# Experts' results scattered to token rows and loaded as plain rows, and a third pair of score banks

## The reference

```python
x = _layernorm(x + _L0_attn_ref(x, ...))            # 16 heads of 64, causal
x = _layernorm(x + _L0_xattn_ref(x, ctx, mask, ...))
x = _layernorm(x + _L0_ffn_ref(x, ...))             # 8 experts, 2 for each token
x = _layernorm(x + _L1_attn_ref(x, ...))            # 16 heads of 16, causal, gates, rotations, an inner MLP
x = _layernorm(x + _L1_xattn_ref(x, ctx, ctx, ...))
x = _layernorm(x + _L1_ffn_ref(x, ...))

def _L0_ffn_ref(x, gate_w, dense_1_w, dense_1_b, dense_2_w, dense_2_b):
    gate = xf @ gate_w
    weights, sel = jax.lax.top_k(gate, k=2)
    weights = jax.nn.softmax(weights, axis=-1)
    h = swiglu(jnp.einsum('ecd,td->tec', dense_1_w, xf) + dense_1_b[None])
    y = jnp.einsum('edf,tef->ted', dense_2_w, h) + dense_2_b[None]
    y_sel = jnp.take_along_axis(y, sel[:, :, None], axis=1)
    return jnp.einsum('tkd,tk->td', y_sel, weights)
```

## Time and profile before

| | |
|---|---|
| median of 3 runs | 1195.58 us (1195.24 to 1195.78) |
| the profiled execution, its own time | 1197.88 us |
| its span, first to last instruction | 1196.1 us |
| busy: PE, DVE, ACT, POOL | 1098.9, 718.9, 551.1, 474.6 us |
| mean granted clock of TensorE | 0.97 of full speed |
| first block / experts / last block | about 0 to 474 / 474 to 699 / 699 to 1196 us |

### The profile page before, as it was taken

How to read it: one execution, slowest core, us unless ns; L and a number is a source line. 1 busy time by engine, 2 the same in 40 slices (tenths; PEclk the granted TensorE clock), 3 DMA queues, 4 the chain that set the end, 5 groups by cost and what they waited for, 6 DMA issues and landing times. The chain is left out here.

```text
span 1196.1 us, 20449 instructions
## 1 busy us (share of the span) xinstructions
PE 1098.9 (92%) x6772; PEld 792.6 (66%) x6772; DVE 718.9 (60%) x2197; ACT 551.1 (46%) x1399; POOL 474.6 (40%) x551
## 2 busy tenths in 40 slices
PE   9899989998999897999999988699899999998997
PEld 4476557645754676999999965455555665575875
DVE  1482376247524846555655647749849787956367
ACT  1381255217421834333333328367476557643542
POOL 0160034006400885666666547515432442323023
PEclk9999999999999899999999989589999999999999
DMA  6000200020002014951111135000100100000001
GB/s 209 19 1 1 60 19 2 0 60 19 1 0 61 2 61 144 323 163 46 50 49 45 45 110 185 6 1 9 28 1 17 36 2 26 10 1 19 1 1 36
DMA packets 39997, 55.85 MB, mean 47 GB/s; under 512 B 6758, under 2 KB 32166, under 8 KB 39894
## 3 DMA queue, kind: packets, MB, share of 16 engines
q1 hardware_dynamic: 30598, 39.61, 10.1%
q0 software_dynamic: 3408, 9.31, 2.8%
q10 hardware_dynamic: 5888, 5.64, 1.5%
HBM read 43.76 MB, written 10.78 MB: 46 GB/s over the span
## 5 line engine op out<-in xcount | busy, mean ns | idle before, releaser
L1821 PE MATMUL bank<-words 128*128 128x256 f32 (+3 forms) x872 | 268.3, 459 | 17.7 <-ACT words L2428 3.3
L1821 PEld LDWEIGHTS bank<-words 128*128 128x128 f32 (+1 forms) x872 | 163.9, 194 | 96.0 <-issue 58.9
L464 PE MATMUL bank<-words 128*128 128x512 f32 x384 | 171.1, 594 | 0.2 <-issue 0.2
L409 POOL TENSOR_TENSOR words<-words 128x256 f32<-128x256 f32 (+1 forms) x128 | 102.5, 830 | 152.7 <-DVE words L1090 152.2
L1297 PEld LDWEIGHTS bank<-words 128*128 128x128 f32 x1248 | 145.8, 192 | 3.5 <-ACT words L1333 1.6
L1297 PE MATMUL bank<-words 128*128 128x128 f32 x1248 | 146.3, 276 | 0.9 <-ACT words L1333 0.9
L787 ACT ACTIVATE words<-words 128x128 f32<-128x128 f32 (+1 forms) x256 | 112.9, 443 | 33.5 <-DVE words L923 33.5
L464 PEld LDWEIGHTS bank<-words 128*128 128x128 f32 x384 | 71.0, 190 | 78.5 <-issue 78.2
L779 ACT ACTIVATE words<-bank 128x512 f32<-128x512 f32 x48 | 28.7, 597 | 177.8 <-PE bank L464 177.8
L1348 ACT ACTIVATE words<-words 128x1024 f32 x39 | 41.1, 1057 | 137.1 <-PE bank L1297 113.2
L913 DVE COPY words<-bank 128x512 f32<-128x512 f32 x48 | 33.2, 691 | 91.9 <-PE bank L464 91.6
(11 more groups left out here) (366 smaller groups left out, 2050.8 us busy)
## 6 DMA issues: line engine op xcount, KB each, us to landing
words<-in_w SPq DMA_DIRECT2D x8, 1024.0 KB, 9.9
y_slots<-words ACTq DMA_DIRECT2D x39, 128.0 KB, 1.7
words<-in_w SPq DMA_DIRECT2D x8, 512.0 KB, 10.1
words<-in_x SPq DMA_DIRECT2D x4, 512.0 KB, 4.2
x_rows<-words SPq DMA_DIRECT2D x16, 128.0 KB, 1.8
words<-in_wm SPq DMA_DIRECT2D x2, 1024.0 KB, 7.2
out_x<-words SPq DMA_DIRECT2D x16, 128.0 KB, 1.8
words<-in_xt SPq DMA_DIRECT2D x3, 512.0 KB, 3.9
```

The source lines that it names most:

```text
L409: last = pool.tensor_tensor(part, part, inv[:, j % SLOTS0, :, t:t + 1].to_broadcast([P, 2, P * (t + 1)]), ALU.mult)
L464: last = pe.matmul(bank[c % 2][:, :], w, r, start=k == 0, stop=k == KD - 1)
L1821: last = pe.matmul(out, w, r, start=i == 0, stop=i == len(pairs) - 1)
```

## The change

The results no longer stay in slot order. A new table `home` gives for each slot the row of `y2` to which its result goes: a token's first choice goes to row RETURNED + token, its second choice to 2048 rows further. The one-hot tables carry RETURNED (6144) or RETURNED + 2048 besides the token's number, so `source` is the number's low eleven bits, and empty slots go to rows of their own below RETURNED.

POOL scatters each tile's 128 rows with an indirect transfer, behind `copy_values(j + 2)`; ACT issues no store. The product of gate and sigmoid moves from POOL to DVE. DVE's slot numbers and `base` fall away. At the end of the experts POOL no longer waits for the stores; SP does, at the head of the last block. Rows come back by plain loads of 128 rows on SP's queue, those of groups 0 and 1 early, and POOL's gathers fall away.

In the second half of group 0's attention the units rotate over three pairs of banks, 0 and 1, 2 and 3, 6 and 7. The turned rows of group 1, which had banks 6 and 7, go to banks 5 and 7. The third pair is used in no other place.

```diff
+RETURNED = -(-SLOTS // (B * S)) * B * S
...
-            for v, pattern, step in ((lane, [[1, P]], 0), (number, [[1, SLOT_TILES]], 0), (token, [[P, TILES]], 1), (index, [[1, 1]], 1)):
+            for v, pattern, step in ((lane, [[1, P]], 0), (number, [[1, SLOT_TILES]], 0), (index, [[1, 1]], 1)):
                 pool.iota(v[:, :], pattern=pattern, base=0, channel_multiplier=step, allow_small_or_imprecise_dtypes=True)
+            pool.iota(token[:, :, :], pattern=[[B * S, 2], [P, TILES]], base=RETURNED, channel_multiplier=1, allow_small_or_imprecise_dtypes=True)
...
-                dve.tensor_tensor(keep["base"][:, :], end[:, :], length[:, :], ALU.subtract)
...
-            dve.tensor_copy(keep["source"][:, :], bank[0][:, 0:SLOT_TILES]).then_inc(routed, 1)
+            dve.tensor_copy(keep["source"][:, :], bank[0][:, 0:SLOT_TILES])
+            dve.drain()
+            dve.tensor_scalar(keep["source"][:, :], keep["source"][:, :], B * S - 1, None, ALU.bitwise_and).then_inc(routed, 1)
+            dve.tensor_scalar(owner[:, :], number[:, :], float(P), index[:, 0:1], ALU.mult, ALU.add)
+            dve.drain()
+            dve.scalar_tensor_tensor(owner[:, :], bank[0][:, 0:SLOT_TILES], 0.0, owner[:, :], ALU.is_equal, ALU.mult)
+            dve.drain()
+            dve.tensor_tensor(keep["home"][:, :], bank[0][:, 0:SLOT_TILES], owner[:, :], ALU.add)
             last_shares(0)
...
-                pool.wait_ge(gated, j + 1)
-                pool.tensor_tensor(sig[:, :], gate[:, :], sig[:, :], ALU.mult).then_inc(mixed, 1)
-            pool.tensor_copy(keep["l_at"][:, :, :], keep["slot"][:, :, 0:NT])
+                pool.wait_ge(yread, j + 1)
+                pool.indirect_dma_start(dram["y2"][:, :], bass.IndirectOffsetOnAxis(ap=home[:, j:j + 1], axis=0),
+                                        y[:, j % 2, :], None).then_inc(ystored[j % 2], 16)
             pool.memset(keep["l_minus_half"][:, :, :], -0.5)
...
-            for s in range(2):
-                pool.wait_ge(ystored[s], 16 * ((SLOT_TILES + 1 - s) // 2))
...
-                act.wait_ge(yread, j + 1)
-                act.dma_start(dram["y2"].rearrange("(j p) n -> p j n", p=P)[:, j, :], y[:, j % 2, :]).then_inc(ystored[j % 2], 16)
...
-                dve.tensor_tensor(chosen[:, r, :, :], chosen[:, r, :, :], base[:, :].unsqueeze(1).to_broadcast([P, TILES, NE]), ALU.mult)
-            dve.drain()
-            dve.tensor_reduce(first[:, :, :], chosen[:, :, :, :], AX.X, ALU.add)
-            dve.drain()
-            dve.scalar_tensor_tensor(rank[:, :, :], first[:, :, :], float(P), rank[:, :, :], ALU.mult, ALU.add)
-            dve.drain()
-            dve.tensor_copy(keep["slot"][:, :, :], rank[:, :, :])
...
-                dve.drain()
-                dve.wait_ge(mixed, j + 1)
+                dve.wait_ge(gated, j + 1)
+                dve.tensor_tensor(sig[:, :], gate[:, :], sig[:, :], ALU.mult)
+                dve.drain()
                 dve.scalar_tensor_tensor(hidden[:, s, :], value[:, :], -8.0, sig[:, :], ALU.max, ALU.mult).then_inc(hready, 1)
...
+        def pair_of(g, j):
+
+            return (0, 1, 3)[(j - PAIRS1 // GB) % 3] if g == 0 and j >= PAIRS1 // GB else j % 2
...
+            def load_context(g, following=None):
 
                 if g:
                     sp.wait_ge(xs, GB * g)
                 sp.dma_start(kxt[:, :, :], dram["kx"].rearrange("g p (k n) -> g p k n", k=KD)[g]).then_inc(cloaded, 16)
+                if following is not None:
+                    load_returned(following)
                 if g:
                     sp.wait_ge(xav, 4 * g)
                 sp.dma_start(vx[:, :, :], dram["vx"].rearrange("g p (b n) -> g p b n", b=GB)[g]).then_inc(cloaded, 16)
 
+            def load_returned(g):
+
+                if g >= 2:
+                    sp.wait_ge(vmm, NT * (g - 1) + NT)
+                    sp.wait_ge(qkmm, NT * (g - 1) + NT)
+                for n in (r * NT + t for t in range(NT) for r in range(2)):
+                    first = RETURNED + n // NT * B * S + (NT * g + n % NT) * P
+                    sp.dma_start(returned(g, n), dram["y2"][first:first + P, :]).then_inc(backed[g % 2][n % NT], 16)
+
+            for s in range(2):
+                sp.wait_ge(keep["ystored"][s], 16 * ((SLOT_TILES + 1 - s) // 2))
+            load_returned(0)
             for g in range(G - 1):
...
+            load_returned(1)
...
+                if p == 1:
+                    load_returned(2)
                 if z is not None:
-                    load_context(z + 1)
+                    load_context(z + 1, 3 if p == 2 else None)
...
-            def gather(g):
-
-                if g > 0:
-                    pool.tensor_copy(at[:, :, :], keep["slot"][:, :, bass.ts(g, NT)])
-                    pool.drain()
-                for n in (r * NT + t for t in range(NT) for r in range(2)):
-                    pool.indirect_dma_start(returned(g, n), None, dram["y2"][:, :],
-                                            bass.IndirectOffsetOnAxis(ap=at[:, n // NT, n % NT:n % NT + 1], axis=0)).then_inc(backed[n], 16)
...
-                if b == 0:
-                    gather(1)
...
-                if a is not None and a + 1 < G:
-                    pool.wait_ge(vmm, NT * a + NT)
-                    gather(a + 1)
...
+                if g == 0 and first >= PAIRS1 // GB + 1:
+                    first = max(first - 1, PAIRS1 // GB)
                 if first >= 1:
                     pe.wait_ge(s1e, PAIRS1 * g + first)
                 for part, keys, queries in ((slice(0, S), 0, slice(b * S, (b + 1) * S)),
                                             (slice(S, S + P), P, slice(b * S + P, (b + 1) * S))):
-                    for n in (2 * (j % 2) + o for j in units for o in range(2)):
+                    for j, o in ((j, o) for j in units for o in range(2)):
+                        n = 2 * (j % 2) + o
                         r = slice(32 * n, 32 * n + 32)
                         k0 = m * GT + b * S + keys
-                        last = pe.matmul(bank[n][:, part], ktm[r, odd, k0:k0 + P], qt[r, m, queries], start=True, stop=True)
+                        last = pe.matmul(bank[2 * pair_of(g, j) + o][:, part], ktm[r, odd, k0:k0 + P], qt[r, m, queries], start=True, stop=True)
                 last.then_inc(s1, len(units))
...
-                for j in range(PAIRS1 // GB + 3):
+                for j in range(PAIRS1 // GB + 3 + b):
                     if j < PAIRS1 // GB:
                         scores(0, (PAIRS1 // GB * b + j,))
-                    if j >= 3 and j % 2:
-                        weighted(0, QUADS1 // GB * b + (j - 3) // 2)
-                    if b and j in (7, 8):
-                        turn(1, n4, j - 7, lambda t: xn[:, t, :], bank[j - 1])
+                    if j >= 3 + b and j % 2 != b:
+                        weighted(0, QUADS1 // GB * b + (j - 3 - b) // 2)
+                    if b and j == PAIRS1 // GB:
+                        turn(1, n4, 0, lambda t: xn[:, t, :], bank[5])
+                    if b and j == PAIRS1 // GB + 1:
+                        pe.wait_ge(s1e, PAIRS1 - 2)
+                        turn(1, n4, 1, lambda t: xn[:, t, :], bank[7])
...
+                act.activation(es[:, j % 4, :, :], pair(pair_of(g, j))[:, :, 0:CAUSAL], ACT.Exp, scale=DH1 ** -0.5).then_inc(s1e, 1)
...
-                dve.wait_ge(backed[n], 16 * g + 16)
+                dve.wait_ge(backed[g % 2][t], 32 * (g // 2) + 32)
...
-                if j in (PAIRS1 // GB, PAIRS1 // GB + 2):
+                if j in (PAIRS1 // GB + 1, PAIRS1 // GB + 3):
                     dve.wait_ge(combined, (j - PAIRS1 // GB) // 2 + 1)
                     front_half(1, (j - PAIRS1 // GB) // 2)
-                if j in (PAIRS1 // GB + 3, PAIRS1 // GB + 4):
-                    front_rows_of(1, j - PAIRS1 // GB - 3)
+                if j in (PAIRS1 // GB + 4, PAIRS1 // GB + 5):
+                    front_rows_of(1, j - PAIRS1 // GB - 4)
...
-    dram["y2"] = nc.dram_tensor("y2_slots", (SLOTS, D), F32, kind="Internal").ap()
+    dram["y2"] = nc.dram_tensor("y2_rows", (RETURNED + 2 * B * S, D), F32, kind="Internal").ap()
```

51 lines of the change are left out of this document (23 added, 28 removed).

## The result

The changed kernel takes 1203.4 us (median of 5 runs, 1201.12 to 1204.68) against 1195.78 for the kernel before (5 runs); the ratio of the runs is 1.0044, 95% interval 1.0025 to 1.0062. In a second comparison it was 1.0034 (1.0022 to 1.0046), with 11 and 16 runs. So it is slower by 4 to 5 us. The forecast was 1197.2, its range 1192.8 to 1202.5. The median lies 0.9 us above that range; but the kernel before took up to 1200.4 us in these runs too, and the ratio, on the 1195.58 us that the forecast started from, gives 1200.8, inside the range. The number alone decides little; what the loss is made of was not what the prediction said. The profiled execution took 1204.68 us, span 1202.9, so 6.8 us more than that of before.

What follows compares the result with a forecast made beforehand. PE was taken to bound the experts' stretch, a chain from PE to DVE to ACT the first group's attention. Terms 0.75 + 2.6 + 0.1 + 0.3 - 2.1 = +1.65 us on 1195.58 gave 1197.2, range 1192.8 to 1202.5.

Steps and rivals of the forecast that it cites:

- number 4: End of the experts: DVE's product adds 0.4, the barrier needs only the last scatter's issue; +0.1 us, ends -0.4 and +0.6.
- 1. Routing: Behind the owners' table: four small DVE operations more, one less, ahead of the barrier; +0.75 us, ends 0 and +1.3.
- 2. Steady tiles: Experts' tiles: POOL's scatter, gather and copy fit into the 5.52 us step, so no cost.
- 3. While the weights arrive: Weight bursts: gathers behind scatters land late, costing 1.7 us at tile 4, then 0.2 and 0.7; +2.6, ends 0.5 and 6.5.
- The term of 0.8 for the scatter ahead: First weight burst: extra landing time of a gather with the scatter's rows ahead of it; 0.8 us, between 0 and 3.7.
- rival C: Weight bursts: strict one-queue reading, fifth tile lands 4.6 us late, sum about +5, 1200.6 us; chance 0.18.
- 5. Rows back: Rows to tokens: plain loads stay hidden, POOL's sums move beside DVE's chain to the first scores; +0.3 us.
- 6. Third pair: Second half of the first group's attention: less waiting for scores with three bank pairs; -2.1 us, ends -1.0 and -4.0.
- Rival D: Every experts' tile: scatter and gather land too late even with idle DMA queues; +26, about 1222 us; chance 0.07.
- 0.36 for slower by over 0.2%: Whole kernel: chance of a loss over 2.4 us, from rival C, Rival D and about a quarter of the small-loss forecast.

Runs made afterwards that it cites:

- e1: Changed kernel with POOL's two memsets and drain moved ahead of its experts loop, nothing behind the last scatter: 1198.8 us, ratio 1.0007 to the kernel before.
- e9: e1 with one POOL drain more, at tile 20 of the 40, after POOL's copy and ahead of its wait for the result: 1198.9 us, one run.
- e4: Kernel before with a POOL drain put behind the last of the second group of eight gathers of results: 1201.95 us, one run.
- e12: e11 with the gather issued ahead of the wait for the tile's result and its scatter, the drain directly behind the gather: 1209.99 us, ratio 1.0101.
- e13: e12 with the drain moved to the head of tiles 8 to 38, directly behind the previous tile's scatter and ahead of POOL's copy: 1214.1 us, ratio 1.0130.
- e11: e10 with POOL waiting for DVE's last weighted sum's pair of the first half before adding the second group's second half of rows: 1194.85 us, ratio 0.9973.
- e5: Kernel before with the third pair of score banks alone, results still stored and gathered: 1197.52 us against 1198.9, ratio 0.9992.
- e14: e13 without the third pair of score banks, the scores taking turns in two pairs again: 1215.0 us, ratio 1.0143 to the kernel before.
- e16: e12's order with the drain only in every fourth tile from 8 to 36, behind POOL's copy and ahead of the gather: 1193.71 us, ratio 0.9947.
- e10: e1 with a POOL drain in each of tiles 8 to 37, after POOL's copy and ahead of its wait for the result: 1195.0 us, ratio 0.9972.

## Why the prediction was wrong in its mechanism

The failed step is number 4, "now it needs only the issue of the last scatter": +0.1 us forecast with the last tile, +6.5 measured (0.49 in the last tile, where +0.4 was forecast, and 5.97 at the barrier, where -0.3 was). The landing was indeed no longer waited for: with no drain behind the last scatter PE needs 3.05 us from its last products to the next block instead of 4.84 (e1). What stood in its place was POOL's drain, which I read in the diff as a line that stays where it was. It did stay, but what is queued ahead of it changed: 39 scatters were added to 36 gathers, the last of them directly ahead, and a drain pays about 0.083 us for each since the last one (e1, e9) and waits for what has not landed (e4, e12, e13). Before, the same drain had 36 gathers, the last issued 21 us earlier; by the same price, an estimate, it took some 3.1 us from 694.07, so until 697.2, hidden by the last store's landing at 699.1. The trace of the kernel before held a hint that the prediction does not use: POOL's 0.82 us of idle time, counted as issue, ahead of L1712, at a drain behind eight gathers.

The other steps, in order.

1. Routing: +0.75 forecast, +0.96 at the stage's start: right. Half of it came back at once, as the first products of the experts ran at a clock that rose earlier: over their first 1.75 us the granted clock was 0.98, before 0.69 over 1.71 us, and L1302's first 32 took 3.86 us, before 4.33. The prediction had no term for that.

2. Steady tiles: 0 and 0. The scatter takes 0.99 us, the gather 0.98 instead of 1.46, both under my 1.46. e9 showed more slack than I had worked out: a scatter 2 us late cost nothing.

3. While the weights arrive: +2.6 forecast, +0.73 measured; the mechanism was right (e12 takes the delay away by order alone), the size was not. The turn of tile 4 (499.52) came almost without the gap of 1.7 us that was forecast, since its gather, issued at 493.22, had landed in 6.3 us; the next turn and one in the second burst were 0.3 us late each. The term of 0.8 for the scatter ahead does not show: with a scatter issued 1.3 us ahead of them the three gathers of the bursts landed in 6.3 to 6.6 us, and four of the kernel before, at other moments of the same bursts and with no scatter ahead, in 6.0 to 7.3. That also answers the rule of the Trainium skill ("DMA: Bandwidth & Descriptors", on SWDGE, HWDGE and iDMA) in its strict reading, rival C: one queue for both did not add the 3.7 us of it.

4. Above.

5. Rows back: +0.3 forecast. The rows were hidden behind the context products, as I said. The stretch up to the first scores gave 0.31 back, and the one behind them, with the sums beside DVE, cost 1.55, so +1.2 in all. I had bounded this at +1.4 by three operations of one kind (L3043), and it was another, the pair of scans, that took 1.8 us more (3.22 for 1.41). e11 shows POOL's part.

6. Third pair: -2.1 forecast, -2.4 in the ledger, 1.6 to 1.7 of it by the pair itself (e5, e14). Right in mechanism and place; the rest of the 2.4 is not the third pair's.

That the ratio puts the time inside the range is luck. The range reached so far up only for the bursts, which cost 1.9 us less than forecast; the drain, which no term or rival held, used up that room. Without the 5.97 us of the barrier the ledger would end at +0.8. Rival C gave nearly the right time (1200.6) for a reason that is refuted. Rival D did not happen: 5.52 us in every tile. The chances: 0.36 for slower by over 0.2% was where the result fell, but none of the cases named its cause.

## What to carry to other kernels

When a diff adds transfers to a queue, look for every drain and barrier behind them on the same engine, also those that the diff does not touch: the profile shows a drain only as idle time put down to "issue", to the sequencer, or to another engine's wait. Here it paid to take POOL's drain away from the place behind 75 indirect transfers, to drain now and then where POOL had slack, and not directly behind a transfer. And follow a wait that is taken away to the next one of the same kind: in e1 PE won 7.8 us at the barrier and lost 5.5 of them again some 20 us later.

## What the runs showed of the hardware

- A POOL drain costs about 0.083 us for each indirect transfer since the last drain, also when all have landed: 6.37 us for 75, 3.01 for 34. Whether transfers or their rows count is open, as all had 128 rows; a direct transfer was not tried. Why there is such a price is open too.
- Directly behind an indirect transfer a drain held POOL for 2.25 us (gathers, e4), 2.6 to 3.8 (gather, e12) and 2.3 to 3.8 (scatter, e13). That is more than the landing: in the tile of e12 shown above the gather landed 2.8 us after its start, and POOL went on 0.87 us later, where the price for two transfers would be 0.3. How the two add up is open.
- A scatter of 128 rows of 1 KB: 0.96 to 1.0 us on POOL, landing 2.4 us after its start, 6.7 in the burst of weights. The page "Perfetto Trace Analysis" of the Trainium skill, section on the DMA instruction by GPSIMD, says that the profiled end is that of writing the descriptors and not of moving the data; the rows agree (0.96 and 2.4).
- The gather of the experts took 0.98 us in the changed kernel and 1.46 before. From 485 us on, all 35 gathers of the kernel before ran beside DVE's operation on the hidden rows (L1397); in the changed kernel none of the 35 gathers and 39 scatters ran beside a DVE operation that reads and writes SBUF alone. In e16 six gathers behind drains took 1.50, and all six ran beside such operations (L1395, L1397). But e12 has transfers of 1.0 us beside the same two, so the neighbour alone does not decide it; no run moved it by itself.
- PE's granted clock: 0.50 for 5.4 us after a gap of 2.86 us (kernel before), 0.55 over 5.75 us after one of 8.82 (changed kernel), and 1.00 over 5 us after one of 1.06 (e1). The quicker barrier of e1, e9, e10 and e16 so brought 1.8 us by itself and some 3 us by the clock (10.28 for 13.26).
